# Graph layer on one core: four edges in a row on 112 partitions, and the last nodes' x turned and multiplied by W1 at the start

## What is computed

```
agg = segment_sum(edge_attr, dst)             # (6250, 128)
h   = relu(concat([x, agg, u]) @ W1 + b1)     # W1: 272 x 256; u is one row for all nodes
out = h @ W2 + b2 + x                         # W2: 256 x 128
result = layernorm(x + out)                   # over the 128 features, eps 1e-5
```

## Time and profile before

| | us |
|---|---|
| median of 3 runs | 185.27 |
| lowest, highest | 185.25, 185.79 |
| the profiled execution, its own time | 185.73 |
| its span in the profile | 184.0 |
| TensorE busy | 154.1 (84%) |
| VectorE busy | 115.4 (63%) |
| ScalarE busy | 51.5 (28%) |
| GpSimd busy | 25.4 (14%) |
| read from HBM, written | 58.50 MB, 3.20 MB |

### The profile page before, as it was taken

The page is one execution under the profiler, slowest core; times in us unless marked ns, Lnnn a source line. Parts: engine busy times, 40 slices in busy tenths (PEclk is TensorE's granted clock), DMA queues, the critical chain, the costliest instruction groups (busy, mean ns, idle before and its releaser), DMA issues.

```text
span 184.0 us, 5378 instructions
## 1 busy us (share of the span) xinstructions
PE 154.1 (84%) x2195; PEld 113.9 (62%) x2195; DVE 115.4 (63%) x369; ACT 51.5 (28%) x110; POOL 25.4 (14%) x29
## 2 busy tenths in 40 slices
PE   0056979979979979969979999899889799899970
PEld 0046855955955956845846858467458568677850
DVE  6847499568376385485495466954933745877371
ACT  2021233223323313313313343133133241233230
POOL 7800030110200200200200204002003230000000
PEclk9999999999999999999999999999999999999997
DMA  5999999999999999999999999999999999998011
GB/s 119 315 352 373 374 375 373 371 373 374 374 374 373 375 372 373 376 372 373 374 373 374 375 373 374 375 373 360 363 374 374 371 374 370 367 398 303 11 43 33
DMA packets 42196, 62.07 MB, mean 337 GB/s; under 512 B 1975, under 2 KB 39541, under 8 KB 42170
## 3 DMA queue, kind: packets, MB, share of 16 engines
q1 hardware_dynamic: 41046, 61.23, 95.0%
q10 hardware_dynamic: 1124, 0.48, 1.2%
HBM read 58.50 MB, written 3.20 MB: 335 GB/s over the span
## 4 chain that ended last, share of the span: by engine, by line
PE 44%; DMA 39%; SPq 8%; DVE 4%; ACT 1%; issue 1%; DVEq 0%
DMA edge_ring<-in_edge_attr_dram 37%; PE sum_ps L845 17%; PE turn_ps L867 7%; PE hid_ps L907 6%; PE hid_ps L900 6%; PE out_ps L920 5%; SPq L276 4%; SPq L291 3%; DMA base_row<-in_dst_dram 2%; DVE bases L568 2%; PE xt_ps L920 1%; PE xt_ps L882 1%; DVE local_rows L576 1%; ACT local_t L429 1%; PE xt_ps L834 1%
## 5 line engine op out<-in xcount | busy, mean ns | idle before, releaser
L845 PE MATMUL sum_ps<-edge_ring,onehot 128*32 128x128 f32 x1662 | 58.5, 284 | 13.0 <-DMA edge_ring<-in_edge_attr_dram 10.8
L845 PEld LDWEIGHTS sum_ps<-edge_ring,onehot 128*32 128x32 f32 x1662 | 45.2, 113 | 27.9 <-DMA edge_ring<-in_edge_attr_dram 13.3
L630 DVE TENSOR_TENSOR agg_t<-agg_t,turn_ps 128x128 f32 x70 | 20.2, 288 | 56.7 <-PE turn_ps L867 52.6
L594 DVE TENSOR_TENSOR onehot<-iota,local_t 128x768 f32<-128x768 f32 (+1 forms) x40 | 33.6, 843 | 3.0 <-ACT local_t L429 2.4
L402 POOL TENSOR_TENSOR x_all<-x_all,half_b 128x512 f32<-128x512 f32 (+3 forms) x16 | 17.7, 1115 | 127.4 <-PE xt_ps L882 127.4
L466 ACT ACTIVATE hid_t<-hid_ps,bias 128x512 f32<-128x512 f32 (+3 forms) x32 | 18.1, 584 | 37.1 <-PE hid_ps L907 37.1
L867 PE MATMUL turn_ps<-place,sums 128*128 128x128 f32 (+1 forms) x140 | 26.5, 306 | 0.0
L907 PE MATMUL hid_ps<-agg_t,w_a 128*128 128x512 f32 (+3 forms) x64 | 24.1, 500 | 0.6 <-DVE agg_t L630 0.5
L867 PEld LDWEIGHTS turn_ps<-place,sums 128*128 128x128 f32 (+1 forms) x140 | 18.9, 192 | 8.0 <-issue 7.9
L920 PE MATMUL out_ps<-w_sb,hid_t 128*128 128x128 f32 (+1 forms) x176 | 21.9, 275 | 0.0
L441 ACT COPY sums<-sum_ps 128x256 f32<-128x256 f32 (+2 forms) x40 | 13.6, 341 | 25.9 <-PE sum_ps L845 25.9
(11 more groups left out here) (64 smaller groups left out, 73.0 us busy)
## 6 DMA issues: line engine op xcount, KB each, us to landing
edge_ring<-in_edge_attr_dram SPq DMA_DIRECT2D x69, 768.0 KB, 12.1
x_all<-in_x_dram SPq DMA_DIRECT2D x10, 256.0 KB, 10.5
out_dram<-x_all SPq DMA_DIRECT2D x1, 2304.0 KB
dst_rows<-in_dst_dram SPq DMA_DIRECT2D x1, 384.0 KB
x_all<-in_x_dram SPq DMA_DIRECT2D x1, 384.0 KB, 11.1
out_dram<-x_all SPq DMA_DIRECT2D x3, 128.0 KB
out_dram<-x_all SPq DMA_DIRECT2D x1, 256.0 KB
w_x<-in_L_gnn_W_dram ACTq DMA_DIRECT2D x1, 128.0 KB, 5.9
```

The lines of the kernel that those rows point to most:

```text
L594: nc.vector.tensor_tensor(onehot[0:ROWS, b % BUFFERS, 0:k * TILES], cols, loc, ALU.is_equal).then_inc(onehot_ready, 1)
L630: nc.vector.tensor_tensor(to, to, turn_ps[b % 2][:, i * SPAN:(i + 1) * SPAN], ALU.add).then_inc(group_added, 1)
L845: last = nc.tensor.matmul(bank[c * WIN:(c + 1) * WIN], onehot[0:p, b % BUFFERS, i * TILES + c * R + r], edge_ring[0:p, slot, c * R + r], s ...
```

## The change

- R = 4 and ROWS = 112: a window is 448 edges, four neighbours (2048 bytes) on each of 112 partitions. A group is 1792 edges in 16 tiles, 896 KB in one DMA. There are 59 whole groups and a rest of 522 edges (one whole window and 74 edges). The ring has 10 slots.
- `complete_at` is a new table; `single0` is 52, so eight groups stand alone at the end (52 to 59), not ten.
- x of the last 1130 nodes is loaded before the first edges (and all destinations before it), turned, and multiplied by `w1_x` at the start; ScalarE keeps the products in SBUF (`x_hid_late`). `w1_x` is the first weight that is loaded.
- For these pieces `sum_hidden_a` starts its bank anew, VectorE adds `x_hid_late` and the bank (`add_x_hidden`, two additions for a piece), and relu reads the sum from SBUF.
- The written-out order of the last batches is replaced by loops over `hidden_step` and `out_step`. In VectorE's late steps normalisation stands ahead of the step's one-hot, and the additions behind the moments.
- The least allowed base of each group comes from one reduction instead of nine maxima.

```diff
-R = 3
+R = 4
...
-ROWS = 128
+ROWS = 112
...
-SLOTS = 12
+SLOTS = 10
...
+COMPLETE_AT = [6, 10, 16, 20, 26, 30, 36, 40, 44, 50, 52, 54, 57, 58, 59]
...
-    complete_at = [6, 12, 18, 24, 30, 36, 40, 46, 52, 58, 60, 63, 66, 67, 69, n_grp]
+    complete_at = COMPLETE_AT + [n_grp]
...
-    single0 = 60
...
+    single0 = complete_at[LAST] + PAIR
...
-    hidden_step = [batch_first.index(complete_at[n]) for n in range(n_big)]
+    late_step = batch_first.index(single0)
+    hidden_step = [batch_first.index(complete_at[n]) for n in range(n_pieces)]
+    hidden_step[A] = max(hidden_step[A], late_step + 1)
...
-            load_group(0)
+                                 ).then_inc(x_landed[2], 16)
             sp.wait_ge(pad_set, 1)
-            sp.dma_start(dst_rows[64:full_grp], dst_full[64:full_grp]).then_inc(dst_landed, 16)
-            sp.dma_start(dst_rows[full_grp:n_grp, 0, 0:rest_edges],
+            sp.dma_start(dst_rows[pad0:full_grp], dst_full[pad0:full_grp]).then_inc(dst_landed, 16)
+            sp.dma_start(dst_rows[full_grp:n_grp].rearrange("g c e -> g (c e)")[:, 0:rest_edges],
                          dst[full_grp * EDGES_GRP:n_edges].rearrange("(o e) -> o e", o=1)).then_inc(dst_landed, 16)
-            for g in range(1, n_grp):
+            load_x_late()
+            for g in range(n_grp):
...
+            act.dma_start(w1_x[:], w1[0:d, :]).then_inc(w1_x_landed, 16)
...
+            def copy_x_late(k):
+                act.wait_ge(x_turned, k + 1)
+                at = 0
+                for n in late_parts[k]:
+                    _, p, j = pieces[n]
+                    last = nc.scalar.copy(x_t_late[:, late_cols_of(n)].rearrange("f (p j) -> f j p", j=j),
+                                          late_turned[k][:, at:at + p * j].rearrange("f (j p) -> f j p", j=j))
+                    at += p * j
+                last.then_inc(x_t_ready, 1)
+            def keep_x_hidden(k):
+                act.wait_ge(late_x_summed, k + 1)
+                for m in range(m_chunks):
+                    last = nc.scalar.copy(x_hid_late[:, m, late_col[k]:late_col[k] + late_cols[k]], late_hidden[k][m])
+                last.then_inc(late_x_ready, 1)
+            for k in range(n_late):
+                copy_x_late(k)
+            keep_x_hidden(0)
...
+            for k in range(1, n_late):
+                keep_x_hidden(k)
...
+                    if late:
+                        act.wait_ge(late_added, m_chunks * (n - n_big) + m + 1)
+                    else:
+                        act.wait_ge(hidden_summed, m_chunks * n + m + 1)
...
+                    src = x_hid_late[:, m, late_cols_of(n)] if late else hidden_bank(n, m)
                     nc.scalar.activation(hid_t[:, n % 2, m, 0:p * j].rearrange("h (j p) -> h j p", j=j),
-                                         hidden_bank(n, m).rearrange("h (p j) -> h j p", j=j), ACT.Relu,
+                                         src.rearrange("h (p j) -> h j p", j=j), ACT.Relu,
...
+            def add_x_hidden(n):
+                dve.wait_ge(hidden_summed, m_chunks * (n + 1))
+                if n == A:
+                    dve.wait_ge(late_x_ready, n_late)
+                for m in range(m_chunks):
+                    xh = x_hid_late[:, m, late_cols_of(n)]
+                    nc.vector.tensor_tensor(xh, hidden_bank(n, m), xh, ALU.add).then_inc(late_added, 1)
...
-            late_step = batch_first.index(single0)
...
-            b = late_step
-            step(b)
-            step(b + 1)
-            moments(LAST)
-            step(b + 2)
-            normalize(LAST)
-            step(b + 3)
-            moments(A)
-            step(b + 4)
-            normalize(A)
-            step(b + 5)
-            moments(B)
-            step(b + 6)
-            normalize(B)
-            step(b + 7)
-            step(b + 8)
-            moments(C_)
-            step(b + 9)
-            normalize(C_)
+            for b in range(late_step, n_batch):
+                for n in range(LAST, n_pieces):
+                    if out_step[n] + 2 == b:
+                        normalize(n)
+                step(b)
+                for n in range(LAST, n_pieces):
+                    if out_step[n] + 1 == b:
+                        moments(n)
...
+                for n in range(A, E):
+                    if hidden_step[n] == b:
+                        add_x_hidden(n)
...
+            add_x_hidden(E)
+            add_x_hidden(REST)
...
+            def turn_x_late(k):
+                pe.wait_ge(x_landed[k], 32 if k == n_late - 1 else 16)
+                if k == 1:
+                    pe.wait_ge(x_landed[0], 16)
+                at = 0
+                for n in late_parts[k]:
+                    _, p, j = pieces[n]
+                    for jj in range(j):
+                        last = nc.tensor.transpose(late_turned[k][:, at:at + p], x_all[0:p, x_slot[n] + jj],
+                                                   ident[0:p, 0:p])
+                        at += p
+                last.then_inc(x_turned, 1)
+            def sum_x_late(k):
+                pe.wait_ge(x_t_ready, n_late if k == n_late - 1 else k + 1)
+                for m in range(m_chunks):
+                    last = nc.tensor.matmul(late_hidden[k][m], w1_x[:, m * P:(m + 1) * P],
+                                            x_t_late[:, late_col[k]:late_col[k] + late_cols[k]], start=True, stop=True)
+                last.then_inc(late_x_summed, 1)
+            pe.wait_ge(consts_ready, 3)
+            for k in range(n_late):
+                turn_x_late(k)
+            pe.wait_ge(w1_x_landed, 16)
+            sum_x_late(0)
...
+            pe.wait_ge(x_t_ready, n_late)
+            for k in range(1, n_late):
+                sum_x_late(k)
...
+            def sum_hidden_a(n):
                 node0, p, j = pieces[n]
                 late = n >= n_big
-                if not late:
-                    pe.wait_ge(x_t_ready, n + 1)
-                    if n > 0:
-                        pe.wait_ge(hidden_ready, m_chunks * n)
-                else:
-                    pe.wait_ge(x_t_ready, len(x_parts))
-                    pe.wait_ge(hidden_ready, m_chunks * max(n - 1, n_big))
-                for m in range(m_chunks):
-                    src = x_t_late[:, node0 - late0:node0 - late0 + p * j] if late else x_t[:, n % 2]
-                    nc.tensor.matmul(hidden_bank(n, m), w1_x[:, m * P:(m + 1) * P], src,
-                                     start=(m == 0 or not late), stop=False, skip_group_check=late)
-            def sum_hidden_a(n):
-                node0, p, j = pieces[n]
                 pe.wait_ge(group_added, complete_at[n])
+                if late:
+                    pe.wait_ge(hidden_ready, m_chunks * n_big)
+                    if n >= B + 1:
+                        pe.wait_ge(late_added, m_chunks * (n - 1 - n_big))
                 for m in range(m_chunks):
                     nc.tensor.matmul(hidden_bank(n, m), w1_a[:, m * P:(m + 1) * P], agg_t[:, node0:node0 + p * j],
-                                     start=False, stop=True, skip_group_check=n >= n_big).then_inc(hidden_summed, 1)
+                                     start=late, stop=True).then_inc(hidden_summed, 1)
...
-            b = late_step
-            sum_batch(b)
-            turn_batch(b - 1)
-            sum_out(LAST)
-            turn_x(n_big + 2)
-            sum_batch(b + 1)
-            turn_batch(b)
-            sum_hidden_x(A)
-            sum_hidden_a(A)
-            sum_batch(b + 2)
-            turn_batch(b + 1)
-            sum_out(A)
-            sum_hidden_x(B)
-            sum_batch(b + 3)
-            turn_batch(b + 2)
-            sum_hidden_a(B)
-            sum_batch(b + 4)
-            turn_batch(b + 3)
-            sum_out(B)
-            sum_batch(b + 5)
-            turn_batch(b + 4)
-            sum_hidden_x(C_)
-            sum_batch(b + 6)
-            turn_batch(b + 5)
-            sum_hidden_x(D)
-            sum_hidden_a(C_)
-            sum_batch(b + 7)
-            turn_batch(b + 6)
-            sum_out(C_)
-            sum_hidden_a(D)
-            sum_batch(b + 8)
-            turn_batch(b + 7)
-            sum_out(D)
-            sum_hidden_x(E)
-            sum_batch(b + 9)
-            turn_batch(b + 8)
-            sum_hidden_x(REST)
-            turn_batch(b + 9)
+            for b in range(late_step, n_batch):
+                sum_batch(b)
+                turn_batch(b - 1)
+                for n in range(LAST, E):
+                    if out_step[n] == b:
+                        sum_out(n)
+                for n in range(A, E):
+                    if hidden_step[n] == b:
+                        sum_hidden_a(n)
+            turn_batch(n_batch - 1)
```

199 lines of the change are left out of this document (95 added, 104 removed).

## The result

The changed kernel takes **280.74 us** (median of 4 runs, 275.85 to 287.64), the kernel before 185.44 us in the runs beside them: **1.497 times as long, 95% interval 1.480 to 1.515**. The direction was forecast, the size not at all.

What follows compares the result with a forecast made beforehand. The stream of edges up to 144.55 us, then a 35.9 us tail set by the order of TensorE, VectorE and ScalarE, bound the kernel. +1.4 - 2.8 + 0.5 + 0 + 3.2 = +2.3 us on 185.27 gave 187.5 us, range 183.5 to 197.

Steps and rivals of the forecast that it cites:

- Packets of 2048 bytes: Stream of edges: four edges in a row move 382.5 GB/s instead of 374, -2.8 us; the ends give -10.6 and +6.1.
- bytes: Stream up to group 51: 93,184 edges instead of 92,160, 0.52 MB more, +1.4 us at 374 GB/s.
- 112 partitions: Stream, lower end of the rate: 7/8 of 408 = 357 GB/s if proportional to partitions; the skill's ports cap it at 381.
- The start of TensorE: Before the first sum: larger set-up and late x by W1 move it from 15.40 to 17.9 us.
- the price of 0: Late start of TensorE: caught up by about group 27, so nothing reaches the end, 0 us.
- my +0.5: Start of the stream: an empty queue while loads wait for a memset costs +0.5 us, bounds -0.3 and +1.5.
- TensorE never catches up: Rival on the start: waits for other engines take the 1.2 us gained in ten groups; 2.5 us more, 190.0 us, chance 0.10.
- The tail: From group 51's landing to the last normalisation: 39.1 us after for 35.9 before, +3.2 us.
- the walk: Step-by-step count of the tail's three engines: waits of some 7 us and 2.3 at the end outweigh 6 saved on TensorE.
- The sign that I named for the walk: In the tail: TensorE waits of 1 to 3 us each, with VectorE busy nine tenths, would show the count right.
- the tail stays at 35.9: Rival on the tail: VectorE's additions and late normalisations hide in its waits for TensorE; 184.3 us, chance 0.08.
- By partitions at 357: Rival on the stream: the rate goes by partitions, 357 GB/s, +6.1 us for -2.8; 196.5 us, chance 0.20.

Runs made afterwards that it cites:

- r4_p128: Kernel after, with each whole group's load widened from 112 to 128 partitions, 14% more bytes of edges read: 210.06 us.
- r4_rows35: Kernel after, with each window's 448 edges loaded as 128 rows of 3.5 edges, first ten groups widened with extra bytes; sums not the reference's: 198.07 us.
- r3_p112: Kernel before, with only partitions 0 to 111 of each whole group loaded and summed, an eighth of the edges left out: 234.18 us.
- late_alone: Kernel before plus the late half alone: late x turned and multiplied at the start, added on VectorE in the tail, with the tail's loops: 192.42 us, ratio 1.0335.
- late_opt: late_alone with the tail's orders for TensorE, VectorE and ScalarE written out by hand, aggregate products a group behind their additions: 184.44 us, ratio 0.9947.

## Why the prediction was right or wrong

- **What bounds before**: right. The stream to 144.55 and then the order of three engines; both halves of the change were felt in these two stretches.
- **Packets of 2048 bytes** (382.5 GB/s): right in size, on 128 partitions. 386 in r4_p128, 381 in r4_rows35 with 1792 bytes. The **bytes** (+1.4 us) are a count; no run measures them alone.
- **112 partitions**: the step that failed, and with it some 86 of the 93 us of error (group 51's sum at 230.20 where my terms put it at 143.7). I bounded the rate from below by 7/8 of 408, in proportion to the partitions (and from the stores' rate; from the loads' own 374 it would have been 327). The only row that I had, 181 GB/s on 64 partitions, said that half of the partitions have half of the rate; it didn't say that the points between lie on a line. They don't: 128 partitions have 374 GB/s, 120 have 214 to 280, 112 have 224 to 252 (288 at the start of r3_p112), 96 have 222 to 238. It is a step, and leaving out one sixteenth of the partitions costs a quarter of the rate or more. The estimate by the Trainium skill's ports, 381, was off in the same way: it counts the ports that a transfer reaches, and measured were 224 to 252. What decides is which partitions a load covers; by what mechanism stays open.
- **The row that would have warned me** was in the trace and I used it as an end point only: a load on 64 partitions in a block, at a covered share (1.09) and half the rate, where loads of edges on 128 partitions reach 373 at 1.06. A share at full with a rate at half means that each packet takes about twice as long. A line through that point was one reading; that 112 in a block might share the fault was another, and it had no price.
- **The start of TensorE**: first sum at 20.77, not 17.9 (21.2 in r4_rows35, 19.2 in r4_p128, 18.9 in late_alone). My own terms, 1.0, 1.7 and 0.4, come to 3.1 ahead of ScalarE's copies and not to the 2.5 that I used. And I took the turning and the first product as hidden: TensorE waited 7.7 us for the late x, and the destinations, which before were first at 9.12, came behind it:

```profile
12.81 0.21 PE L883 MATMUL out_ps<-ident,rel 60*4 60x60 f32 x1
```

- **What the late start costs**: the price of 0 was nearly right for late_alone, where group 59's sum ends 1.1 us late. In r4_rows35 group 51's sum stands at 147.66, where my terms gave 143.7, and these 4.0 us aren't TensorE's alone, as that sum still waited for edges. The bytes of edges up to it, divided by the rate, leave 19.0 us at the front in r4_rows35 (49.02 MB at 381), 19.0 in r4_p128 (54.53 at 386) and 18.4 before (47.19 at 374): an estimate by which the stream starts 0.6 us later, for my +0.5, and loses nothing more. With the bytes of the kernel after, 47.71 MB, the same estimate lands group 51 at 144.2. But TensorE, busy 19.6 to 20.0 us of 20, was ready, as it ran, at 146.75. So the change's own share of the 4.0 lies between 0.6 and 3.1 us, and the rival "TensorE never catches up" (2.5 us) is neither shown nor excluded: the slack that I reckoned, 1.2 us in ten groups, isn't to be seen.
- **The tail**: its waits came as walked. Predicted 1.2, 1.7 and 3.2 us for A's outputs, B's and C's products; measured 1.38, 1.39 and 3.31 in r4_rows35, 1.24, 1.39 and 2.50 in the kernel after. The tail was 45.6 us and not 39.1 for two terms that the walk lacked. Behind the waits TensorE's clock is down: the instructions from 163.91 to 168 and from 175.11 to 181.9 take some 4.7 us longer than at the full clock. And the last group has two windows where every other has four: its 16 matmuls take 2.74 us, where the price of a whole group would give 0.5; with four windows 32 take 1.08. The sign that I named for the walk, a VectorE nine tenths busy, was wrong: it is busy 15.8 us of the 30 from 160 to 190 in r4_rows35, since it waits for ScalarE's roots (2.3 us) and for TensorE (11.6) in turn. The chain between the three engines holds the tail, not the load of one: late_opt has the same work in another order and needs 9 us less.
- **The rivals**: that the tail stays at 35.9 fell with late_alone. By partitions at 357 was the one that pointed the right way, with a fifth of the chance and a fraction of the price. Rates under 357 had 0.08, outside the range and without a price.
- **The sum**: with the rate taken out, 187.5 + 4.0 + 6.5 = 198.0, and r4_rows35 has 198.07. This only says that no stretch is forgotten, since both terms are read from that run; up to 3.4 of the 4.0 are its own extra bytes.

## What to carry to other kernels

The rate of these loads doesn't follow the number of partitions: one load over all 128 is fast, and 120, 112 or 96 in a block mostly lose a quarter to two fifths of it, so change the row length before you change the number of rows (112). r4_rows35, with 3.5 edges on 128, shows that for the rate alone; its sums would need another layout of the tiles. Where a trace shows the DMA engines covered and the rate down, read it as packets that each take longer, and measure the new shape before building on it. Work taken off a busy engine is a gain only if the order behind it puts no long wait in its place, which can cost twice, by itself and by the clock after it; here ordering the tail anew brought all of the gain, about 1 us of 185, with the late half or without.

## What the runs showed of the hardware that I had not expected

- Rate by shape of the load, in GB/s over windows of 20 us from 60 to 160, DMA share 1.02 to 1.11 in all: 128 partitions 368 to 374 (packets of 1536 bytes), 378 to 381 (1792), 385 to 386 (2048); 120 partitions 251 to 280 (214 from 20 to 40 us); 112 partitions 232 to 252 (1536; 288 from 20 to 40), 228 to 243 (2048); 96 partitions 222 to 238; two halves low and high 227 to 294; two halves even and odd 367 to 375; 64, 32 and 16 rows spread out 288 to 303.
- TensorE's clock in the tail: 1.00 with waits up to 0.5 us (before, late_opt) and behind one of 1.59 us (late_alone), 0.51 behind one of 2.42 us (late_alone). The length of the wait alone doesn't sort the cases: in the middle of late_opt's stream the clock fell with a wait of 1.80 us, and in the kernel before it was 1.00 from 60 to 160 us with a wait of 1.68 at 80.34. At the lower level a product of 256 columns takes 2.07 us and not 1.03 to 1.13.
- Matmuls on 32 columns of the array: 34 ns each when four windows take turns (32 in 1.08 us), 171 ns when two do (16 in 2.74), 140 ns in a single window (6 in 0.84 to 0.85); no run asks why.
